# Gated cross-attention layer on one core: step 0 written out by itself on every engine, key splits of pair 1 in step 1

## The reference

```python
x = x + jnp.tanh(g_xattn[0]) * _L0_xattn_ref(_layernorm(x), ctx_768, Wq, bq, Wk, bk, Wv, bv, Wo, bo)
x = x + jnp.tanh(g_ffn[0]) * _L0_ffn_ref(_layernorm(x), weight_q, weight_scale, bias)
```

## Time and profile before

| what | value |
| --- | --- |
| median of 3 runs | 800.2 us (796.23, 800.2, 801.88) |
| profiled execution | 797.8 us; span of its records 796.0 us, so 1.8 us lie around the span |
| granted TensorE clock | 0.999 of full speed |
| busy: PE, DVE, ACT, POOL | 767.5, 543.6, 607.5, 520.7 us |
| DMA | 177.24 MB, mean 223 GB/s |

### The profile page before, as it was taken

How to read it: one execution, slowest core, us unless ns; L and a number is a source line. 1 busy time by engine, 2 the same in 40 slices (tenths; PEclk the granted TensorE clock), 3 DMA queues, 4 the chain that set the end, 5 groups by cost and what they waited for, 6 DMA issues and landing times.

```text
span 796.0 us, 16271 instructions
## 1 busy us (share of the span) xinstructions
PE 767.5 (96%) x5883; PEld 529.6 (67%) x5938; DVE 543.6 (68%) x863; ACT 607.5 (76%) x846; POOL 520.7 (65%) x546
## 2 busy tenths in 40 slices
PE   9998989999999999999999999999999999999996
PEld 6665566676676676667667676667667667666563
DVE  5967767575686667667676667757568665755568
ACT  5766858787786877968687786778779687787785
POOL 4428465594856758575694957759485675855588
PEclk9999999999999999999999999999999999999999
DMA  8667798878698697869778788787879867666722
GB/s 291 232 196 201 225 288 229 236 228 255 193 283 230 197 271 223 241 199 312 216 194 272 211 266 217 229 258 227 254 195 284 216 183 227 199 174 178 207 64 106
DMA packets 115199, 177.24 MB, mean 223 GB/s; under 512 B 35888, under 2 KB 45488, under 8 KB 113072
## 3 DMA queue, kind: packets, MB, share of 16 engines
q1 hardware_dynamic: 88336, 128.14, 52.4%
q10 hardware_dynamic: 26784, 48.06, 22.7%
HBM read 120.03 MB, written 56.13 MB: 221 GB/s over the span
## 4 chain that ended last, share of the span: by engine, by line
PE 83%; issue 4%; DVE 4%; DMA 3%; ACT 2%; POOL 2%; SPq 1%; ACTq 0%; DVEq 0%; POOLq 0%
PE bank_b L432 28%; PE bank_a L432 18%; PE scores L487 8%; PE sum_ps L538 7%; PE scores L530 6%; PE pv_ps L542 6%; PE bank_a L586 4%; PE bank_b L586 2%; PE bank_a L561 1%; PE scores L432 1%; DMA k_rows<-k_parts 1%; SPq L235 1%; DVE row_max L1288 1%; PE sum_ps L502 1%; DMA wk_stage<-in_wk 1%
## 5 line engine op out<-in xcount | busy, mean ns | idle before, releaser
L1288 DVE TENSOR_REDUCE row_max<-scores 128x16 f32<-128x1920 f32 x64 | 137.9, 2154 | 15.4 <-PE scores L487 15.2
L1662 POOL TENSOR_TENSOR o_lo<-on,o_hi 128x512 fp32r<-128x512 f32 x48 | 62.8, 1309 | 112.2 <-ACT o_hi L962 112.2
L942 ACT ACTIVATE probs<-scores 120x2048 f32<-120x2048 f32 x64 | 120.1, 1877 | 20.5 <-PE scores L530 20.4
L1317 DVE SCALAR_TENSOR_TENSOR q_parts<-bank_b,bq_c,q_parts 128x512 fp32r<-128x512 f32 x45 | 33.8, 750 | 135.7 <-ACT q_parts L895 135.7
L487 PEld LDWEIGHTS scores<-k_sb,q_sb 32*128 32x128 f32 x1952 | 60.0, 186 | 54.2 <-issue 41.5
L1670 POOL TENSOR_TENSOR x<-x,gbias_r 128x512 f32<-128x512 f32 x64 | 83.0, 1298 | 17.4 <-ACT cen L968 16.3
L1656 POOL TENSOR_TENSOR x<-x,gbo_r 128x512 f32<-128x512 f32 x64 | 82.0, 1292 | 5.1 <-DMA x<-in_x 5.0
L1620 POOL TENSOR_TENSOR xt<-xt,rstd_b 128x512 f32<-128x512 f32 x56 | 85.3, 1561 | 0.0
L1675 POOL TENSOR_TENSOR x<-x,u_sb 128x512 f32<-128x512 f32 x56 | 72.6, 1296 | 6.8 <-DVE u_sb L1393 6.6
L432 PE MATMUL bank_b<-xt_hi,wq_hi 128*128 128x512 f32 x188 | 75.2, 400 | 0.0
L487 PE MATMUL scores<-k_sb,q_sb 32*128 32x120 f32 x1952 | 71.2, 282 | 3.3 <-ACT q_sb L873 2.3
(11 more groups left out here) (246 smaller groups left out, 1947.2 us busy)
## 6 DMA issues: line engine op xcount, KB each, us to landing
q_stack<-q_rows ACTq DMA_DIRECT2D x180, 256.0 KB, 4.5
q_rows<-q_parts SPq DMA_DIRECT2D x60, 512.0 KB, 5.6
xt<-in_x_t SPq DMA_DIRECT2D x16, 1024.0 KB, 8.2
x<-in_x SPq DMA_DIRECT2D x64, 256.0 KB, 4.6
out_x<-x SPq DMA_DIRECT2D x61, 256.0 KB, 3.1
x_in<-in_x SPq DMA_DIRECT2D x60, 256.0 KB, 5.4
k_stack<-k_rows SPq DMA_DIRECT2D x90, 120.0 KB, 4.8
k_rows<-k_parts SPq DMA_DIRECT2D x30, 240.0 KB, 3.2
```

Of the source, the lines that this page charges most:

```text
L942: act.activation(probs[0:KEYS], scores[0:KEYS], ACT.Exp, scale=SCALE).then_inc(p_ready, 1)
L1288: dve.tensor_reduce(row_max[:].rearrange("p (t r) j -> p r t j", r=ROWG)[:, :, :, j], scores[:, :, 0:QT * KEYS].rearrange("p r (t k) -> p ...
L1662: pool.tensor_tensor(o_lo[i % 2][j], on[:], o_hi[i % 2][j].bitcast(F32), ALU.subtract).then_inc(o_split, 1)
```

## The change

Every engine gets a function `first_step` that stands in place of `step(0)`; `step` loses its branches for i == 0 and gains some for i == 1. SP has no such function; its list ahead of step 1 is written anew.

- PE: the projection of query group j + 1 now stands behind the by-query scores of group j, and the projections of keys and values behind the by-key scores. Banks change accordingly; the fold uses bank_a.
- ACT: `split_high0(2)` stands before the first `bias_q`, the split of Wo in quarter one, `bias_k` behind `split_high` of groups 1 and 3. No split of pair 1's keys is left in step 0.
- DVE: `x_statistics(2, 0)` and `(2, 1)` move from the prologue into the step, `split_low0(2)` in front of the first `split_low`, `split_low0(3)` behind `scale_q1(2)`, and further statistics between `scale_q1`, `split_low` and `maxima`.
- POOL: `low_wo` stands ahead of `low_k(0, 2)`, `scale_x(2, ...)` ahead of `low_k(0, 3)`.
- SP: query stores come earlier in its list, the stores of pair 0's tiles 2 and 3 later; rstd and the context of the next pair are loaded ahead of the residuals of batch 0.
- All four splits of pair 1's keys, their stores, and both halves of `stack_k(2, ...)` are in step 1, at other places than those of later steps.

The diff, cut to these parts:

```diff
@@ sync, ahead of step 1
             load_x(2, 2)
+            store_q(1, 0)
             load_x(2, 3)
-            store_q(1, 0)
-            store_k(0, 2)
             load_x(3, 0)
+            store_q(1, 1)
             load_x(3, 1)
             store_rstd(2)
+            store_k(0, 2)
             load_rstd(2)
-            store_q(1, 1)
-            store_k(0, 3)
             load_x(3, 2)
             load_x(3, 3)
+            store_q(1, 2)
+            store_k(0, 3)
+            load_x(4, 0)
             stack_k(1, 1)
-            store_q(1, 2)
-            store_k(1, 0)
-            load_x(4, 0)
             store_rstd(3)
             store_q(1, 3)
-            store_k(1, 1)
+            load_x(4, 1)
+            load_ctx(2)
+            load_rstd(3)
...
@@ tensor
+            def first_step():
+                pe.wait_ge(max_done, nth(0, DT, 3))
+                scores_by_key0(0)
+                pe.wait_ge(v_ready, nth(1, 1))
+                project_q(1, 0, bank_b)
+                attend(0, 0)
+                scores_by_query(1, 0)
+                project_q(1, 1, bank_a)
+
+                pe.wait_ge(max_done, nth(1, DT, 0))
+                scores_by_key0(1)
+                pe.wait_ge(q_split, nth(0, DT, 0))
+                project_k(1, 0, bank_b)
+                project_k(1, 1, bank_b)
+                attend(0, 1)
+                scores_by_query(1, 1)
+                pe.wait_ge(k_ready, nth(1, DT, 1))
+                project_q(1, 2, bank_b)
+
+                pe.wait_ge(max_done, nth(1, DT, 1))
+                scores_by_key0(2)
+                pe.wait_ge(q_split, nth(0, DT, 1))
+                project_v(2, bank_a)
+                attend(0, 2)
+                scores_by_query(1, 2)
+                pe.wait_ge(v_ready, nth(2, 1))
+                project_q(1, 3, bank_a)
...
+                pe.wait_ge(log_done, nth(0, DT, 3))
+                turn_max(1, sum_ps)
+                fold_bias(bank_a, range(DT - 1, DT))
@@ scalar
+            def first_step():
+                exponentials(0, 0)
+                split_high0(2)
+                bias_q(1, 0, bank_b)
+                split_high(1, 0)
+                log_sums(0, 0)
+                invert_sums(0, 0)
+                act.wait_ge(wo_gated, 1)
+                act.activation(flat(wo_hi), flat(wo_stage), ACT.Copy).then_inc(wo_hi_done, 1)
+                high_o(0, 0)
...
             def step(i):
...
                 spread_max(i)
+                if i == 1:
+                    split_high_k(1, 0)
...
                 invert_sums(i, 1)
+                if i == 1:
+                    split_high_k(1, 1)
...
                     integers(m, 1)
+                if i == 1:
+                    split_high_k(1, 2)
...
                 high_o(i, 3)
-                if i == 0:
-                    split_high_k(1, 1)
+                if i == 1:
+                    split_high_k(1, 3)
@@ vector
+            def first_step():
+                scale_q1(0, bank_b)
+                split_low0(2)
+                x_statistics(2, 0)
+                split_low(1, 0, bank_b)
+                maxima(1, 0)
+                normalise_o(0, 0)
+
+                scale_q1(1, bank_a)
+                x_statistics(2, 1)
+                x_statistics(2, 2)
+                split_low(1, 1, bank_a)
+                x_statistics(2, 3)
+                maxima(1, 1)
+                normalise_o(0, 1)
+
+                scale_q1(2, bank_b)
+                split_low0(3)
...
@@ gpsimd
+            def first_step():
+                low_wo(slice(0, 1))
+                low_o(0, 0)
+                low_wo(slice(1, DT))
+                x_rstds(2)
+                low_k(0, 2)
+                low_o(0, 1)
+                pool.wait_ge(qk0_split, nth(DT - 1, 2, 1))
+                for c in range(DT):
+                    scale_x(2, c)
+                low_k(0, 3)
+                low_o(0, 2)
+                x_rstds(3)
+                low_o(0, 3)
...
             def step(i):
...
                     x_rstds(f)
+                if i == 1:
+                    low_k(1, 2)
...
                 low_o(i, 3)
-                if i == 0:
-                    low_k(1, 1)
+                if i == 1:
+                    low_k(1, 3)
```

More of the change, by code:

```diff
@@ L401, in step @@
                     store_q(b, 3)
+                if i > 1 and is_batch(b):
                     stack_k(b, 1)
@@ L723, in step @@
                     quantised_layer(m, 1, bank_a)
-                if keys_next and i > 0:
+                if keys_next:
                     project_k(pair, 2, bank_a)
@@ L828, in _ @@
             pe.wait_ge(wk_lo_done, CT)
-            step(0)
+            first_step()
             pe.wait_ge(wo_lo_done, 2)
@@ L1008, in copy_zt @@
                 act.activation(zt[:].rearrange("p t c s -> p (t c s)"), bank[:].bitcast(BF16), ACT.Copy).then_inc(zt_ready, 1)
+            def first_step():
[8 more added lines that the diff above has]
+                high_o(0, 0)
+                exponentials(0, 1)
+                bias_q(1, 1, bank_a)
+                split_high(1, 1)
+                bias_k(1, 0, bank_b)
+                bias_k(1, 1, bank_b)
+                log_sums(0, 1)
+                invert_sums(0, 1)
+                split_high0(3)
+                split_high_k(0, 2)
+                high_o(0, 1)
+                exponentials(0, 2)
+                bias_q(1, 2, bank_b)
+                split_high(1, 2)
+                stack_q(1, 0)
+                copy_v(2, bank_a)
+                log_sums(0, 2)
+                invert_sums(0, 2)
+                split_high_k(0, 3)
+                high_o(0, 2)
+                exponentials(0, 3)
+                bias_q(1, 3, bank_a)
+                split_high(1, 3)
+                stack_q(1, 1)
+                bias_k(1, 2, bank_b)
+                bias_k(1, 3, bank_b)
+                high_x(2, 0)
+                log_sums(0, 3)
+                invert_sums(0, 3)
+                high_x(2, 1)
+                high_max(1)
+                high_x(2, 2)
+                high_x(2, 3)
+                copy_max(1, sum_ps)
+                high_o(0, 3)
             def step(i):
@@ L1080, in step @@
                     quant_round(m, 1)
-                if i == 0:
-                    bias_k(pair, 2, bank_a)
-                    bias_k(pair, 3, bank_a)
                 high_o(i, 2)
-                if is_batch(k_of(i)):
-                    split_high_k(k_of(i) // 2, 2 * (i % 2) + (i > 0))
+                if i > 1 and is_batch(k_of(i)):
+                    split_high_k(k_of(i) // 2, 2 * (i % 2) + 1)
                 if is_batch(m):
@@ L1232, in _ @@
             high_ctx(1)
-            for i in range(0, LAST):
+            first_step()
+            for i in range(1, LAST):
                 step(i)
@@ L1394, in dequantise @@
                                          op0=ALU.mult, op1=ALU.mult).then_inc(u_ready, 1)
+            def first_step():
[14 more added lines that the diff above has]
+                split_low0(3)
+                x_statistics(3, 0)
+                x_statistics(3, 1)
+                split_low(1, 2, bank_b)
+                maxima(1, 2)
+                normalise_o(0, 2)
+                scale_q1(3, bank_a)
+                x_statistics(3, 2)
+                gate_rows()
+                x_statistics(3, 3)
+                split_low(1, 3, bank_a)
+                maxima(1, 3)
+                low_max(1)
+                normalise_o(0, 3)
+                low_x(2, 0)
+                fold_rows(bank_a)
+                low_x(2, 1)
+                low_x(2, 2)
+                low_x(2, 3)
+                dve.tensor_copy(flat(w8_b), w8_stage).then_inc(rows_ready, 1)
+                dve.wait_ge(rows_ready, 1)
             def step(i):
@@ L1442, in step @@
                     x1_statistics(m, 1)
-                if i > 0 and is_batch(f):
+                if is_batch(f):
                     x_statistics(f, 2)
```

132 lines of the change are left out of this document (44 added, 88 removed).

## The result

The changed kernel takes 791.27 us (median of six runs, 790.52 to 792.0), the kernel before beside it 797.89 (795.88 to 801.88): a ratio of 0.9912, 95% interval 0.9885 to 0.9939. The profiled execution is 791.26 us with a span of 789.4, against 797.8 and 796.0. The forecast was 796.0 with a range of 790 to 802, so the range held, but the time lies where rival A put it (793.4 from a median of 800.2) and not at the forecast.

The account below looks back on a forecast made before the run. TensorE is busy nearly throughout, so only its stalls can be won: 3.9 us in step 0 plus 0.3 in step 1 make 4.2 off 797.8, giving 793.6, scaled to a median of 796.0; range 790 to 802.

Parts of the forecast that it names:

- rival A: Step 1's stalls go too, loads filling the idle DMA stretch, first key store landed by 99.3; gain 6.8, median 793.4; chance 0.22.
- The 0.83: Step 0, TensorE's stall before by-query scores at 45.49: goes, as two statistics move behind the scaling and q_sb comes 1.05 earlier.
- The 1.45: Step 0, TensorE's stall before by-query scores at 67.00: goes, as 5.2 us of TensorE work cover scaling, exponentials, bias and split.
- The 0.48: Step 0, TensorE's stall for the probabilities at 63.62: goes with the long copy of Wo, moved to the first quarter.
- The rule that the prediction weighed: VectorE with two SBUF inputs and GpSimd reading SBUF alternate by whole instructions; group 3's split loses up to 1 us, sum unchanged or 0.5.
- it lands at 100.7, and TensorE stands 1.4 us: Step 1, key store that ScalarE's second key split awaits: lands behind 3568 KB; TensorE stall 1.4 us, bounds 0 and 6.3.
- the 1.71 becomes 1.2: Step 1, TensorE's stall at 110.96: shrinks to 1.2 as GpSimd's deviations and the quantisation come late; bounds 0 and 1.7.
- the limit of 99.3: Step 1: latest start of ScalarE's second key split without delaying attention, 103.2 before, now 3.9 earlier.
- rival C: Key stores landing over 9.4, 8.4 and 3.6 us after issue decide step 1; 6.3 us lost, median 806.5; chance 0.11.
- The second and third waits: Step 1, ScalarE's third and fourth key splits, at about 112 and 125.0: their stores land in time, no wait.
- the 0.2 before step 2: End of step 1: the fourth key split itself puts 0.2 us before step 2's first exponentials.
- B: Step 1 is bound by the queue and gives step 0's gain back; gain 0 to 1, median 799.7; chance 0.15.

Follow-up runs that it names:

- experiment 11: Changed kernel with the statistics of batch 2's first two x tiles put back ahead of the gating of Wo on VectorE; 791.75 us in one run.
- experiment 12: Changed kernel with VectorE's small split for group 3 put back in front of the scaling of query group 2; 790.93 us in one run.
- experiment 9: Changed kernel with TensorE's old order in step 0 put back, the other engines as changed; 799.21 us, ratio 1.0007.
- experiment 10: Kernel before with VectorE's order alone changed: two batch 2 statistics and the split of group 3 moved behind scalings; 800.87 us, ratio 1.005.
- experiment 5: Changed kernel, rstd and residual loads held until step 1's first exponentials end, xt load moved behind step 1's first key store; 791.56 us, ratio 0.9914.
- experiment 1: Kernel before with one SP line moved: store of pair 1's key tile 1 behind the residual, context, rstd and xt loads; 795.36 us, ratio 0.9963.
- experiment 3: Changed kernel with rstd, residual and xt loads held until step 1's first exponentials end, about 82.2 us; 798.41 us, ratio 1.0007.
- experiment 2: Changed kernel with SP's x tile, context, rstd, residual and xt loads held until step 1's first query projection; 797.04 us, ratio 0.9988.
- experiment 7: Changed kernel with splits and stores of pair 1's first two key tiles back at step 0's end, step 1 in old order; 801.1 us, ratio 1.0047.
- experiment 8: Changed kernel, pair 1's first two key splits back in step 0, step 1 in old order, key tile 1's store behind xt load; 796.85 us, ratio 0.9994.

## Why the prediction was right or wrong

**The base.** The gain was forecast at 4.2 and measured at 6.6. Of the 4.7 us between 796.0 and 791.27 the other 2.3 is the base: the forecast was scaled to a median of three runs, 800.2, and the median of six is 797.89. On the scale of the profiled execution the forecast was 793.6, against 791.26. A change of 0.88% was told from none with an interval of 0.61 to 1.15%, a little finer than the 1% that the prediction allowed for.

**Step 0: right in size, in part for other reasons.** 3.9 was forecast, 4.13 came; the floor summed from pitches was 39.65, the step took 39.81. The 0.83 went with the two statistics, as said (experiment 11 puts 0.82 back). The 1.45 was put down to the 5.2 us of cover from TensorE's new order; in fact either order takes it away, TensorE's with VectorE's split put back (experiment 12) and VectorE's without TensorE's (experiments 9 and 10). The 0.48 is absent from experiment 9, where the copy of Wo is in the first quarter, and present as 0.50 in experiment 10, where it is not; that fits the named reason. What TensorE's order adds is that no stall takes their place: without it the step loses 4.0 to other waits (experiment 9). That VectorE's order alone brings new stalls (experiment 10) the prediction didn't say. The x tile whose landing was put at 54.2 was read at 54.18 without a wait, and the maxima behind it waited for TensorE.

VectorE met GpSimd as said: the split of group 3 began 0.13 after GpSimd's split of o and took 1.71 us, where its like took 0.68 (the split of group 2, at 43.97). The sum didn't change, since the maxima behind it still waited 1.34 for TensorE. The rule that the prediction weighed (the Trainium skill, "SBUF — State Buffer", section "SBUF: two separate sides") agrees with this row too.

**Step 1: the mechanism was right, the size was not.** The step that failed is the first one there: "it lands at 100.7, and TensorE stands 1.4 us", with its follower "the 1.71 becomes 1.2". The second split did wait for the store, the store did wait for the bytes ahead of it (experiment 5), and the limit of 99.3 was about right: a split at 97.37 cost nothing (experiment 5), and the one at 105.37, less the stall of 5.67, puts the limit at 99.7. But both numbers behind the 100.7 were off. The loads were put at "about 82.4 on"; they went out at 79.80, as soon as rstd's store, issued at 73.61, had landed. The prediction shows no row for 82.4. It fits the bias fold for which the residuals wait on SyncE (82.20 in experiment 1): the fold ends at about 82.3 in the kernel before and at 78.6 in the changed one, so the time seems to have been left where the old step 0 ended; that is inferred. And one rate, 195 KB per us, was taken for the queue in every state. It was 3568 KB in 16.8 us, or 212, in the changed kernel, and 3568 in 23.1, or 154, with loads from 82.17 (experiment 3). Put at the issue time of the forecast, the store lands at 105.3, TensorE stands 5.67 and the gain is nil; put at the real one, nothing is lost. The forecast of 796 stands between these two and describes neither; the bounds of that term, nothing and 6.3, hold both. The lower bound of -12 for the whole step is not worked out there: the bounds given with its terms make -5.1, and rival C's waits about -10.

The second and third waits were forecast at nothing and are nothing; the 0.2 before step 2 is 0.27. SyncE's new waits cost nothing, as said. What the prediction used only as an issue time was the wait that left SyncE: its removal causes 2.5 of the 3.3 us that step 1 gains, and experiment 1 shows it in one line.

**Rivals.** A came true, by its own reason: the loads go out into the stretch that was idle before, and the store lands at 96.6, by 99.3. Rival C's condition, a landing over 9.4 us after issue, is met in the first of its three places in experiment 3, and a loss follows: 5.0 us by its rule, 5.67 measured. What its price lacked is the stretch at half clock. B did not happen: step 2 starts 7.0 earlier, at 122.02.

## What to carry to other kernels

An engine that issues DMAs in order is a queue of its own: before pricing bytes, look for the wait at which it stands and count what stands behind it. A small store that someone waits for goes ahead of a large load that nobody needs yet; here that one line was worth 7 us when the loads were late, and nothing when they were not. Write the landing of a queued transfer as two times, for the earliest and the latest issue, each with a rate read from a stretch in that state; where a wait's limit lies between them, the forecast is one of two outcomes, not their mean.

## What was not expected of the hardware

How steeply a landing grows. The DMA answers of the changed kernel for 84 to 88 and for 88 to 92 us (q1 is SyncE's queue, q10 ScalarE's; then packets, MB, share):

```profile
DMA packets 537, 1.63 MB, mean 408 GB/s; under 512 B 56, under 2 KB 56, under 8 KB 432
...
q1 hardware_dynamic: 526, 1.61, 103.0%
q10 hardware_dynamic: 11, 0.02, 1.4%
...
DMA packets 573, 1.22 MB, mean 306 GB/s; under 512 B 50, under 2 KB 50, under 8 KB 548
...
q10 hardware_dynamic: 350, 0.65, 56.4%
q1 hardware_dynamic: 221, 0.56, 44.1%
```

And of experiment 3 for 88 to 92:

```profile
DMA packets 365, 0.86 MB, mean 215 GB/s; under 512 B 33, under 2 KB 33, under 8 KB 336
...
q1 hardware_dynamic: 190, 0.53, 65.2%
q10 hardware_dynamic: 175, 0.33, 43.6%
```

The engines are busy in all three stretches. SyncE's queue, nearly alone, moved 1.61 MB in 4 us; with ScalarE's loads of q_stack beside it, it moved a third of that. In the changed kernel the residuals and part of xt are through before those loads, issued at 84.12, begin to move; in experiment 3 they meet them. That fits a landing that grows faster than the delay, but the other queue is not all of it. In experiment 3 SyncE's queue moved little from 84 to 88 already, when hardly anything was beside it:

```profile
q1 hardware_dynamic: 502, 0.91, 88.7%
q10 hardware_dynamic: 58, 0.11, 9.4%
```

All packets of that stretch are under 8 KB; of the fast one's, 105 (537 less 432) are not. Whether the size of the packets or the second queue makes a stretch slow was not tried separately and stays open.

TensorE's clock after a stall. In six stalls of 3.00 to 5.67 us (experiments 2, 3, 7 twice, 8, 9) the granted clock fell to 0.50 and stayed there for some microseconds of the work behind; behind a stall of 2.21 (step 1 of experiment 10) and the shorter ones looked at, 1.90 in experiment 8 and 1.71 in the kernel before, it stayed at 1.00. So a long stall here cost more than its length.
